# Moving the second ffn1's routing into the attention, and sorting its rows by expert with scatters from GpSimd

## The chip, the cores and the metric

The kernel runs on one core of a Trainium2 chip, as one program with one launch. The time is that of the device in microseconds, the median of several runs. TensorE's clock is granted at one of two levels, 1.2 and 2.4 GHz, and the profile gives it as a share of the higher.

## The reference

An activation `x` of 4 sequences of 1024 tokens and 128 features goes through six residual steps, each on a layernorm of `x`:

```python
x = x + 0.5 * L0_ffn(layernorm(x))     # shared GEGLU expert + the best of 8 experts
x = x + mamba(layernorm(x))            # 4 Mamba-2 experts, mixed by a softmax
x = x + 0.5 * L0_ffn(layernorm(x))
x = x + 0.5 * L1_ffn(layernorm(x))     # "ffn1"
x = x + attention(layernorm(x))        # causal, q and k of 16 features, v = the input
x = x + 0.5 * L1_ffn(layernorm(x))     # "ffn1" again, with the same weights

def L1_ffn(x):
    scores, experts = top_k(x @ Wg + bg, 2)          # of 8 experts
    gate = softmax(scores)
    # for each of the two: a = gelu(x @ W1[e] + b1[e]) (even e) or silu (odd e)
    return sum of gate * (a @ W2[e] + b2[e])
```

## The kernel before

**Layout.** The 4096 tokens are 32 tiles of 128 (token `t*128 + p` on partition `p`), 8 groups of 4 tiles. `x` stays in SBUF. Each stage is a block with one program for each engine, and engines wait for each other by semaphores; every engine runs its program strictly in the written order. A block ends when all engines have ended.

**An ffn1 stage** has a routing and an expert pass. `route` (L381) finds the two best experts of all tokens with VectorE instructions over 256 scores a partition, counts each expert's tokens with two matmuls, and gives every pair of token and choice a position: the experts one behind the other, each rounded up to whole slots of 128 rows, 71 slots at most (`SLOTS2`). Then 16 batches (`match_vector`, `match_lanes`, `match_tiles`, `place_tensor`) invert this by one-hot products, so that `slot_token` says for each row of a slot which token it holds, and `slot_row` where its result goes. `experts` (L771) then runs the 71 slots. For slot `s`: GpSimd gathers its 128 rows from `xn_rows` in DRAM (`gather`, L816, an indirect DMA); TensorE turns them (`turn`, L849); ScalarE copies them and the expert's W1 (L895, L890); TensorE multiplies (`up`, L861), VectorE adds the bias (L941), ScalarE and VectorE apply gelu or silu (L907, L910, L951), TensorE multiplies again (`down`, L873), and VectorE adds the bias and writes `y` (L964).

What happens to `y` differs. In the first ffn1 (`by_token`) SyncE stores the slots in order (L836), and the attention fetches the rows by position. In the second, GpSimd scatters each slot's rows into `y_rows` by token (`scatter`, L822), in the same program as the gathers, eight slots behind; VectorE's next `y` in that buffer (4 of them) waits for it. At the end SyncE brings `y_rows` back, VectorE adds the rows with their gates to `x`, and the output is stored (L280, L300).

**The attention** (`attend`, L1003) handles 32 blocks of 128 queries. Step `n` of its hand-written loop has, on each engine, the pieces of several blocks: TensorE scores block n, turns the probabilities of n-2 and mixes n-3; VectorE adds n-4 to `x` and finds the maximum of n; ScalarE copies the turned n-2 and takes the exponential of n. Woven in by tables from step to group: GpSimd fetches (`fetch`, L1111) the first ffn1's rows of a group, 8 gathers; VectorE adds them (`take`, L1160) and takes statistics (L1168, L1172, for group 5 in step 15); GpSimd makes the scale and shift (`deviations`, L1101 to L1107), ScalarE norms (L1324, group 5 in step 16); then turns, projections to q and k. Behind the blocks, the same for the second ffn1: once a group's four blocks are added, in step 4g+7, VectorE's `next_statistics` (L1180, L1184), GpSimd's `next_deviations` (L1129 to L1135), ScalarE's norm in step 4g+9 (L1346), turn, copy, scores and `logits`, and SyncE's store to `xn_rows` (L1089). GpSimd's program is, for g = 1 to 7: half the fetch of group g+1, `deviations(g)`, from g = 3 on `next_deviations(g-3)`, the other half of the fetch; the last three `next_deviations` behind it.

## Time and profile before

| | |
|---|---|
| median of 3 runs | 1868.59 us (1867.08 to 1868.68) |
| span of the profiled execution (first to last instruction) | 1864.5 us |
| the profiled execution's own time | not given apart from its span; what lies around a span is 4.1 us against the median |
| TensorE, VectorE, GpSimd, ScalarE busy | 1538, 1227, 1068, 953 us |
| mean granted TensorE clock | 0.906 |

Engines are named PE (TensorE matmul), PEld (TensorE weight load), DVE (VectorE), ACT (ScalarE), POOL (GpSimd) and SP (SyncE); a name with a q is that engine's sequencer. L816 is line 816 of the kernel before. All positions in time are us from the span's start. "Busy" says that an instruction was under way, not that it bounded anything. Idle time in brackets stands behind the instruction that ended it, with what released it.

### The profile page before, as it was taken

The page shows a single profiled execution, that of the slowest core. Times are in us where ns is not written, and L with a number is a line of the kernel's source. Part 1 is how long each engine was busy: PE and PEld are TensorE (multiplying, and loading weights), DVE is VectorE, ACT ScalarE, POOL GpSimd, SP SyncE. Part 2 cuts the span into 40 slices and gives each one's busy share as a digit, 9 for nine tenths or more (in the row PEclk, how much of TensorE's full clock was granted, in tenths as well). Part 3 has the DMA queues.
Part 4 walks back from the last instruction along what each step waited for, and adds up shares of the span by engine and source line. Part 5 has one row for each costly group of instructions (what it writes and reads, how often), then busy time and mean ns, then how long its engine had stood idle before and what let it go on. Part 6 is the DMA issues. An engine that isn't in the chain of part 4 may idle for free. (4 is left out here: it accounts for less than half of the span.)

```text
span 1864.5 us, 35936 instructions
## 1 busy us (share of the span) xinstructions
PE 1538.4 (83%) x10014; PEld 1275.6 (68%) x10015; DVE 1227.0 (66%) x2746; ACT 952.5 (51%) x1962; POOL 1067.6 (57%) x1408
## 2 busy tenths in 40 slices
PE   5879965799999999999869889646995588469883
PEld 3559962478888888888746589635995367358772
DVE  5535547689899999998655445575675477654556
ACT  2213343687878787877622223334663466345451
POOL 2135751388888888888840347535442563267773
PEclk9999966899999999999979999857998698679997
DMA  7001130000000000000031001421221110011115
GB/s 243 1 23 32 46 104 29 2 3 3 3 2 3 3 3 3 2 3 2 2 131 67 17 26 47 136 79 43 65 65 43 33 47 27 18 30 51 49 49 158
DMA packets 66072, 78.88 MB, mean 42 GB/s; under 512 B 23776, under 2 KB 40448, under 8 KB 65936
## 3 DMA queue, kind: packets, MB, share of 16 engines
q1 hardware_dynamic: 51952, 48.82, 8.4%
q0 software_dynamic: 13856, 28.40, 5.7%
q8 instruction: 64, 1.05, 0.2%
q14 instruction: 72, 0.59, 0.1%
q10 hardware_dynamic: 128, 0.02, 0.0%
HBM read 50.20 MB, written 24.90 MB: 40 GB/s over the span
## 5 line engine op out<-in xcount | busy, mean ns | idle before, releaser
L861 PE MATMUL ps<-gT,w_slot 128*128 128x128 f32 x1760 | 246.2, 284 | 4.0 <-ACT gT L895 2.8
L816 POOL DMA_INDIRECT rows_in<-xn_rows,slot_token x188 | 186.0, 989 | 110.1 <-PE ps L849 57.2
L873 PE MATMUL ps<-w,inner_slot 128*128 x1760 | 235.3, 277 | 2.4 <-DVE inner_slot L951 1.8
L861 PEld LDWEIGHTS ps<-gT,w_slot 128*128 128x128 f32 x1760 | 219.9, 196 | 17.7 <-issue 7.9
L822 POOL DMA_INDIRECT y_rows<-y,slot_row x149 | 162.1, 1088 | 108.5 <-DVE y L958 84.9
L873 PEld LDWEIGHTS ps<-w,inner_slot 128*128 128x128 f32 x1760 | 213.9, 192 | 6.7 <-issue 5.0
L1828 DVE SCALAR_TENSOR_TENSOR xbc<-ps,cw,xbc 128x1021 f32<-128x1021 f32 x132 | 168.2, 1274 | 17.8 <-ACT xbc L1707 15.7
L1582 PE MATMUL ps<-xnT,win 128*128 128x512 f32 x256 | 135.0, 653 | 26.3 <-DVE xbc L1828 21.0
L941 DVE TENSOR_TENSOR hb<-ps,b 128x512 f32<-128x512 f32 x142 | 98.1, 691 | 72.0 <-PE ps L861 66.4
L489 POOL TENSOR_TENSOR oh_slot<-match,tile_of 128x284 bf16<-128x284 bf16 (+1 forms) x48 | 46.5, 969 | 171.0 <-DVE match L470 171.0
L2010 POOL TENSOR_TENSOR xd<-t,xd 128x256 f32<-128x256 f32 x128 | 94.6, 739 | 86.9 <-DVE t L1863 86.9
L1633 PEld LDWEIGHTS ps<-XB,LM 128*128 128x128 f32 x1024 | 136.2, 194 | 6.8
L1633 PE MATMUL ps<-XB,LM 128*128 128x64 f32 x1024 | 129.7, 270 | 0.0
L1843 DVE SCALAR_TENSOR_TENSOR LM<-LM,past 128x512 f32<-128x512 f32 x128 | 122.7, 959 | 0.1
L1989 POOL TENSOR_TENSOR Xw<-XB,wst 128x256 f32<-128x256 f32 x128 | 89.8, 702 | 57.4 <-ACT XB L1748 57.4
L747 ACT ACTIVATE gl<-ps 128x512 f32<-128x512 f32 x64 | 38.2, 597 | 148.7 <-PE ps L701 148.7
L2015 POOL TENSOR_TENSOR y<-xd,sz 128x256 f32<-128x256 f32 x128 | 106.1, 829 | 10.0
L900 ACT ACTIVATE gl<-ps 128x512 f32<-128x512 f32 x78 | 46.6, 597 | 124.4 <-PE ps L865 124.4
L849 PE MATMUL ps<-ident,rows_in 128*128 128x128 f32 x220 | 64.6, 295 | 46.2 <-DMA rows_in<-xn_rows,slot_token 33.9
L1648 PEld LDWEIGHTS ps<-wout,yT 128*128 128x128 f32 x512 | 74.2, 198 | 31.4 <-issue 25.4
L964 DVE TENSOR_TENSOR y<-ps,b 128x128 f32<-128x128 f32 x142 | 41.1, 289 | 81.6 <-DMA y_rows<-y,slot_row 50.3
L1582 PEld LDWEIGHTS ps<-xnT,win 128*128 128x128 f32 x256 | 46.4, 201 | 68.2 <-issue 38.5
(295 smaller groups left out, 3983.0 us busy)
## 6 DMA issues: line engine op xcount, KB each, us to landing
w<-in_L_ffn_W SPq DMA_DIRECT2D x5, 2048.0 KB, 11.4
xn_rows<-xn SPq DMA_DIRECT2D x24, 256.0 KB, 3.4
xn<-y_rows SPq DMA_DIRECT2D x24, 256.0 KB, 4.9
y_rows<-y SPq DMA_DIRECT2D x71, 64.0 KB
rows_in<-xn_rows,slot_token POOLq DMA_INDIRECT x220, 2.6
y_rows<-y,slot_row POOLq DMA_INDIRECT x149, 2.4
right<-rows SPq DMA_DIRECT2D x128, 3.0 KB
xn_rows<-rows SPq DMA_DIRECT2D x8, 256.0 KB, 2.0
```

The costliest lines, as they stand in the source:

```text
L816: nc.gpsimd.indirect_dma_start(k.rows_in[:, q, :], None, k.xn_rows[:, :], bass.IndirectOffsetOnAxis(ap=k.slot_token[:, s:s + 1], axis=0)). ...
L822: nc.gpsimd.indirect_dma_start(kept, bass.IndirectOffsetOnAxis(ap=k.slot_row[:, s:s + 1], axis=0), k.y[:, s % RING, :], None).then_inc(sto ...
L861: ins = nc.tensor.matmul(h1[:, u, b * P:(b + 1) * P], w[:, b * P:(b + 1) * P], k.gT[:, r, :], start=True, stop=True)
L873: ins = nc.tensor.matmul(py[:, q % 2, :], k.inner_slot[:, q % RING, b * P:(b + 1) * P], w_dn[:, ds(e * (FB * D) + b * D, D)], start=(b == ...
L941: V.tensor_tensor(k.hb[:, q, :].rearrange("p (b t) -> p b t", b=FB), h1[:, q, :].rearrange("p (b t) -> p b t", b=FB), bcast(k.b1[:, ds(e * ...
L1582: ins = nc.tensor.matmul(piece(n)[:, half * 512:(half + 1) * 512], m.win[:, e, ZW + blk * P:ZW + (blk + 1) * P], k.xnT[:, seq * SEQ + half ...
L1633: ins = nc.tensor.matmul(bankY[:, hd], M[:, r, h * P:(h + 1) * P], XB[:, x, hd], start=True, stop=True)
L1828: inc(V.scalar_tensor_tensor(out, piece(n)[:, 0:SEQ - back], m.cw[:, c, i:i + 1], out, ALU.mult, ALU.add), tap_done if i < 2 else a["conv"])
L1843: inc(V.scalar_tensor_tensor(heads(M[:, r, :]), heads(L[:, u % 3, :]), LARGE, bcast(past[:, r, :], 1, MH), ALU.min, ALU.mult), b["M"])
L1989: inc(G.tensor_tensor(heads(Xw[:, r, :]), heads(XB[:, u % 4, 0:ZW]), bcast(m.wst[:, c:c + MH], 2, HD), ALU.mult), b["Xw"])
L2010: inc(G.tensor_tensor(xd[:, u % 2, :], t2[:, u % 2, :], xd[:, u % 2, :], ALU.add), b["summed"])
L2015: inc(G.tensor_tensor(y2[:, u % 8, :], xd[:, u % 2, :], sz[:, u % 8, :], ALU.mult), b["y2"])
```

## The change

The routing of the second ffn1 is done group by group inside the attention. The group's scores stay in PSUM; VectorE picks the two experts (`choose`, table CHOOSE, step 4g+13), TensorE counts (`next_ranks`, step 4g+14), VectorE turns the counts into positions (`take_ranks`, `place`, step 4g+15). A position now lies in a region of 4096 rows that each expert has in `sorted_rows`, a new DRAM tensor of 33,792 rows with 129 elements (516 bytes): the normed row, and the number of the row in `y_rows` where its result goes. GpSimd writes the rows with 64 scatters (`send`, 8 for each group); its program in the attention is written out anew. The slot table (expert and first row of each slot) is made by `slot_table` at the end of the attention, with the gates. Rows of a slot that no token fills must hold valid targets: Mamba's SyncE program fills the whole tensor with blank rows beforehand, in 33 transfers.

The second expert pass has no routing and no gathers. SyncE loads slot `s` with one transfer of 128 rows that lie one behind the other, whose start it reads into a register, into one of 16 buffers; up to four loads are under way. The scatter of `y` takes its targets from the last column of the loaded rows. The first ffn1 keeps its routing, with one cast in place of four for the slot table.

```diff
-    for shift in range(4):
-        do(V.tensor_copy(k.slot_expert[:, shift, shift:shift + slots], k.erow[:, 0:slots]))
+    put_experts(k, do, slots)
+def put_experts(k, do, slots):
+    four = k.slot_expert[:, :].rearrange("p (a w) -> p a w", a=4)
+    do(k.nc.vector.tensor_copy(four[:, :, 0:slots], bcast(k.erow[:, 0:slots], 1, 4)))
...
-    RING, LAG, AHEAD, LEADS = 4, 4, 16 if top == 1 else 8, 8
-    gathered = [k.counter(f"slot_gathered{r}", 16, lead=0) for r in range(AHEAD)]
-    stored = [k.counter(f"slot_kept{r}" if by_token else f"slot_stored{r}", 16, lead=0) for r in range(RING)]
+    RING, LAG, AHEAD, LEADS = 4, 4, 16 if top == 1 or sorted_in else 8, 8
+    CALLS = 4 if sorted_in else AHEAD
+    gathered = [k.counter(f"slot_moved{r}" if sorted_in else f"slot_gathered{r}", 16, lead=0) for r in range(CALLS)]
+    stored = [k.counter(f"slot_moved{r}" if by_token else f"slot_stored{r}", 16, lead=0) for r in range(RING)]
...
+                row = k.rows_in[:, s % AHEAD, D:D + 1].bitcast(U32) if sorted_in else k.slot_row[:, s:s + 1]
+                nc.gpsimd.indirect_dma_start(kept, bass.IndirectOffsetOnAxis(ap=row, axis=0),
...
-                if early <= t < slots:
+                if early <= t < slots and not sorted_in:
...
+            if sorted_in:
+                for s in range(slots):
+                    if s >= CALLS:
+                        sp.wait_ge(transposed.sem, transposed.at(s - CALLS + 1))
+                    if s >= AHEAD:
+                        sp.wait_ge(stored[s % RING].sem, stored[s % RING].at((s - AHEAD) // RING + 1))
+                    first = sp.value_load(k.slot_base[0:1, s:s + 1], min_val=0, max_val=SORTED - P)
+                    sp.dma_start(k.rows_in[:, s % AHEAD, :], k.sorted_rows[ds(first, P), :]
+                                 ).then_inc(gathered[s % CALLS].sem, 16)
...
+                pe.wait_ge(gathered[q % CALLS].sem, gathered[q % CALLS].at(n * (AHEAD // CALLS) + q // CALLS + 1))
...
-        NORM2, ROWS2, SCORE2 = ({n + back: g for n, g in AGAIN.items()} for back in (2, 4, 5))
-        END = 4 * NG + 9
+        NORM2, ROWS2, SCORE2, CHOOSE, RANK, PLACE = ({n + back: g for n, g in AGAIN.items()} for back in (2, 4, 5, 6, 7, 8))
+        END = 4 * NG + 12
...
-                for g in range(NG):
-                    wait(sp, next_xn, g + 1)
-                    sp.dma_start(xn_rows[:, g * GRP:(g + 1) * GRP, :], rows2[:, g % 2]).then_inc(next_stored[g % 2].sem, 16)
-                for r in range(2):
-                    wait(sp, next_stored[r], NG // 2)
...
-                for g in range(1, NG):
-                    if g + 1 < NG:
-                        fetch(g + 1, 0)
-                    deviations(g)
-                    if g >= 3:
-                        next_deviations(g - 3)
-                    if g + 1 < NG:
-                        fetch(g + 1, 1)
-                for g in range(NG - 3, NG):
-                    next_deviations(g)
+                def send(g):
+                    wait(pool, labelled, 1)
+                    wait(pool, index_ready, g + 1)
+                    wait(pool, next_xn, g + 1)
+                    for c in range(2):
+                        for j in range(GRP):
+                            G.indirect_dma_start(k.sorted_rows[:, :], bass.IndirectOffsetOnAxis(ap=index[:, g, c, j:j + 1], axis=0),
+                                                 back[:, g, c, j, :], None).then_inc(sent.sem, 16)
+                def fetch_group(g):
+                    fetch(g, 0)
+                    fetch(g, 1)
+                fetch_group(2)
+                deviations(1)
+                fetch_group(3)
+                fetch(4, 0)
+                deviations(2)
+                fetch(4, 1)
+                fetch_group(5)
+                deviations(3)
+                next_deviations(0)
+                fetch_group(6)
+                deviations(4)
+                next_deviations(1)
+                send(0)
+                deviations(5)
+                next_deviations(2)
+                fetch_group(7)
+                deviations(6)
+                next_deviations(3)
+                send(1)
+                deviations(7)
+                next_deviations(4)
+                send(2)
+                next_deviations(5)
+                send(3)
+                next_deviations(6)
+                send(4)
+                next_deviations(7)
+                send(5)
+                send(6)
+                send(7)
+                wait(pool, sent, NG * 2 * GRP)
...
+                def top_expert(c):
+                    do(V.tensor_reduce(best[:, c, :], lg[:, c], AX.X, ALU.max))
+                    do(V.tensor_tensor(eq[:, :, :], lg[:, c], bcast(best[:, c, :], 2, NE), ALU.is_equal))
+                    do(V.tensor_tensor(eq[:, :, :], eq[:, :, :], bcast(k.falling[:, :], 1, GRP), ALU.mult))
+                    do(V.tensor_reduce(low[:, :], eq[:, :, :], AX.X, ALU.max))
+                    do(V.tensor_tensor(sel[:, c], eq[:, :, :], bcast(low[:, :], 2, NE), ALU.is_equal))
+                def take_scores(g):
+                    wait(dve, next_scored, g + 1)
+                    V.tensor_tensor(lg[:, 0], ps_next.rearrange("p (j e) -> p j e", e=NE), bcast(k.bg[:, :], 1, GRP), ALU.add
+                                    ).then_inc(next_kept.sem, 1)
+                def choose(g):
+                    wait(dve, next_kept, g + 1)
+                    top_expert(0)
+                    do(V.scalar_tensor_tensor(lg[:, 1], sel[:, 0], -1e30, lg[:, 0], ALU.mult, ALU.add))
+                    top_expert(1)
+                    V.tensor_tensor(marks[:, 0:GRP, :], sel[:, 0], sel[:, 1], ALU.add).then_inc(marks_ready.sem, 1)
+                    V.tensor_sub(k.small[:, g * GRP:(g + 1) * GRP], best[:, 1, :], best[:, 0, :]).then_inc(weights.sem, 1)
+                def take_ranks(g):
+                    first = k.region if g == 0 else filled
+                    wait(dve, ranked, g + 1)
+                    wait(dve, placed, g)
+                    do(V.tensor_tensor(rank[:, :, :], ranks[:, 0:GRP, :], bcast(first[:, :], 1, GRP), ALU.add))
+                    V.tensor_tensor(filled[:, :], ranks[:, GRP, :], first[:, :], ALU.add).then_inc(placed.sem, 1)
+                def place(g):
+                    do(V.tensor_tensor(chosen[:, :, :, :], sel[:, :, :, :], bcast(rank[:, :, :], 1, 2), ALU.mult))
+                    do(V.tensor_reduce(posf[:, :, :], chosen[:, :, :, :], AX.X, ALU.add))
+                    V.tensor_copy(index[:, g], posf[:, :, :]).then_inc(index_ready.sem, 1)
+                def slot_table():
+                    slots, starts = SLOTS2, k.e8[:, 1, 1:NE]
+                    wait(dve, placed, NG)
+                    do(V.scalar_tensor_tensor(k.n_int[:, :], filled[:, :], float(P - 1), k.region[:, :], ALU.add, ALU.subtract))
...
+                    do(V.tensor_tensor(over[:, :, :], bcast(k.iota[:, 0:slots], 2, NE - 1), bcast(starts, 1, slots), ALU.is_ge))
+                    do(V.tensor_reduce(k.erow[:, 0:slots], over[:, :, :], AX.X, ALU.add))
+                    do(V.tensor_tensor(over[:, :, :], over[:, :, :], bcast(gap[:, 0:NE - 1], 1, slots), ALU.mult))
+                    put_experts(k, do, slots)
+                    do(V.tensor_reduce(k.erow[:, 0:slots], over[:, :, :], AX.X, ALU.add))
+                    do(V.scalar_tensor_tensor(k.slot_base[:, 0:slots], k.iota[:, 0:slots], float(P), k.erow[:, 0:slots],
+                                              ALU.mult, ALU.add))
...
-                for n in range(N + MIX + 1):
-                    if n > MIX:
+                for n in range(END):
+                    if MIX < n <= N + MIX:
                         add(n - MIX - 1)
+                    if group_behind(CHOOSE, n) is not None:
+                        take_scores(group_behind(CHOOSE, n))
+                    if group_behind(PLACE, n) is not None:
+                        take_ranks(group_behind(PLACE, n))
...
+                    if group_behind(PLACE, n) is not None:
+                        place(group_behind(PLACE, n))
+                    if group_behind(CHOOSE, n) is not None:
+                        choose(group_behind(CHOOSE, n))
                 wait(dve, added, N)
+                slot_table()
+                gates()
...
+                def next_ranks(n, g):
+                    wait(pe, marks_ready, g + 1)
+                    wait(pe, added, min(n - MIX, N))
+                    nc.tensor.matmul(ps_rank, k.before[:, :], marks[:, :, :].rearrange("p j e -> p (j e)"), start=True,
+                                     stop=False, skip_group_check=True)
+                    for j in range(GRP):
+                        ins = nc.tensor.matmul(ranks[:, j + 1:, :], k.ones_bf[:, :], bcast(marks[:, j, :], 1, GRP - j),
+                                               start=False, stop=(j == GRP - 1), skip_group_check=True)
+                    ins.then_inc(ranked.sem, 1)
...
+                    wait(pe, next_kept, len([m for m in SCORE2 if m < n + MIX]))
+                    wait(pe, placed, len([m for m in RANK if m < n + MIX]))
...
-                    wait(act, next_stored[r], g // 2)
-                    wait(act, next_turned, g - 1)
                     for j in range(GRP):
                         t = g * GRP + j
-                        ins = A.activation(rows2[:, r, j, :], x[:, t * D:(t + 1) * D], ACT.Identity,
+                        ins = A.activation(back[:, g, :, j, 0:D], bcast(x[:, t * D:(t + 1) * D], 1, 2), ACT.Identity,
...
+            def blank_rows(n):
+                e = n * 8 // NT
+                src = bcast(blank[:, e, :], 1, 8) if e < NE - 1 else blank[:, NE - 1:, :]
+                sp.dma_start(blanks[:, n * 8:(n + 1) * 8, :], src).then_inc(blank_in.sem, 16)
...
                 exponent_rows(n)
+                blank_rows(n)
+            blank_rows(NQ)
...
+SORTED = NE * TOK + 8 * P
...
+def ffn1_second(k, S, out):
+    ffn1_buffers(k, S, 16, D + 1)
+    experts(k, 2, SLOTS2, out=out, sorted_in=True)
```

## Rows read from the trace of the kernel before

**Rows 1.** the page's busy times, share of the span and number of instructions

```profile
PE 1538.4 (83%) x10014; PEld 1275.6 (68%) x10015; DVE 1227.0 (66%) x2746; ACT 952.5 (51%) x1962; POOL 1067.6 (57%) x1408
```

**Rows 2.** stretch table by stage: us, each engine busy, clock, DMA

```profile
290.00:1198.00 908.00, 831.29 (x5106) 671.91 (x5104) 686.49 (x1296) 548.20 (x1056) 595.96 (x843) 0.96 0.06 20
...
1274.00:1430.00 156.00, 145.32 (x1207) 138.94 (x1207) 90.54 (x179) 95.73 (x215) 68.41 (x71) 0.97 0.23 60
1430.00:1606.00 176.00, 120.33 (x674) 92.83 (x674) 100.51 (x386) 91.73 (x203) 88.59 (x131) 0.82 0.13 37
1606.00:1650.00 44.00, 10.82 (x67) 6.24 (x67) 40.53 (x89) 9.16 (x18) 16.64 (x16) 0.50 0.00 0
1650.00:1838.00 188.00, 163.28 (x1207) 142.65 (x1207) 91.95 (x178) 95.95 (x215) 143.37 (x142) 0.98 0.17 50
```

**Rows 3.** waits in the second pass: who waited for whom, us, times, longest

```profile
DVE y L964 <- DMA y_rows<-y,slot_row: 50.3, 51, 1.6
```

**Rows 4.** GpSimd in order of time, second pass: start, duration

```profile
1800.03 0.99 POOL L822 DMA_INDIRECT y_rows<-y,slot_row  x1 [0.30 <-issue]
1801.32 0.97 POOL L816 DMA_INDIRECT rows_in<-xn_rows,slot_token  x1 [0.31 <-issue]
```

**Rows 5.** turns and outputs, first pass, then second: min/median/max ns, first and last

```profile
L849 PE MATMUL ps<-ident,rows_in x71: 272/273/476, 1276.9 to 1418.6; 128*128 128x128 f32 x71
...
L964 DVE TENSOR_TENSOR y<-ps,b x71: 281/290/293, 1286.2 to 1426.1; 128x128 f32<-128x128 f32 x71
...
L849 PE MATMUL ps<-ident,rows_in x71: 272/328/476, 1653.0 to 1828.2; 128*128 128x128 f32 x71
...
L964 DVE TENSOR_TENSOR y<-ps,b x71: 282/291/293, 1661.9 to 1835.5; 128x128 f32<-128x128 f32 x71
```

**Rows 6.** all engines in order of time, routing's end to first turn

```profile
1648.67 0.23 DVE L514 TENSOR_TENSOR slot_row<-erow,rt 128x71 uint32<-128x71 f32 x1
...
1650.35 1.07 POOL L816 DMA_INDIRECT rows_in<-xn_rows,slot_token  x1 [6.46 <-POOLq L88]
...
1652.97 0.48 PE L849 MATMUL ps<-ident,rows_in 128*128 128x128 f32 x1 [8.30 <-DMA rows_in<-xn_rows,slot_token]
```

**Rows 7.** GpSimd in order of time, end of the second pass

```profile
1831.01 0.97 POOL L822 DMA_INDIRECT y_rows<-y,slot_row  x1 [0.30 <-issue]
```

**Rows 8.** the line that reads an expert's number into a register

```profile
L802 PEldq TENSOR_LOAD <-slot_expert x48: 297/364/1129, 141.9 to 1833.3; - x48
```

**Rows 9.** the page's DMA issues: KB each, us from issue to landing

```profile
y_rows<-y,slot_row POOLq DMA_INDIRECT x149, 2.4
...
xn_rows<-rows SPq DMA_DIRECT2D x8, 256.0 KB, 2.0
```

**Rows 10.** VectorE in order of time: last statistics of groups 2, 7; routing step

```profile
1528.78 0.38 DVE L1184 BATCH_NORM_AGGREGATE mv<-stat 128x2 f32<-128x6 f32 x4
...
1597.52 0.38 DVE L1184 BATCH_NORM_AGGREGATE mv<-stat 128x2 f32<-128x6 f32 x4
...
1616.48 0.17 DVE L345 CAST e<-n_int 128x8 f32<-128x8 int32 x1
```

**Rows 11.** the attention's 64 fetches on GpSimd: ns min/median/max

```profile
L1111 POOL DMA_INDIRECT back<-y_rows,pos x64: 940/944/1086, 1431.1 to 1551.6; - x64
```

**Rows 12.** GpSimd in order of time: first and last of two chains of deviations

```profile
1528.07 0.20 POOL L1101 TENSOR_TENSOR rstd<-mv,eps 128x4 f32<-128x4 f32 x1 [2.67 <-DVE mv L1172]
...
1531.64 0.23 POOL L1135 TENSOR_SCALAR shift<-shift 128x4 f32<-128x4 f32 x1
```

**Rows 13.** ScalarE in order of time: the norm of group 5

```profile
1531.83 1.64 ACT L1324 ACTIVATE xn<-x,shift,rstd 128x128 f32<-128x128 f32 x4
```

**Rows 14.** stretch table, blocks of the attention

```profile
1500.00:1600.00 100.00, 86.14 (x548) 69.81 (x547) 67.24 (x268) 66.89 (x152) 45.04 (x72) 0.95 0.13 38
```

**Rows 15.** the casts of the slot table

```profile
L374 DVE CAST slot_expert<-erow x4: 197/198/198, 1645.9 to 1646.6; 128x71 int32<-128x71 f32 x4
```

**Rows 16.** SyncE's issues in Mamba, in order of time

```profile
331.01 2.94 SPq L1966 DMA_DIRECT2D right<-rows  x4
```

More of the change, by code:

```diff
@@ L802, in fetch @@
             _, held = nc.values_load_multi_w_load_instructions(
-                k.slot_expert[0:1, shift, ds(t - behind + shift, count)], engines=(engine,), min_val=0, max_val=NE - 1,
+                k.slot_expert[0:1, ds(shift * WIDE + (t - behind + shift), count)], engines=(engine,), min_val=0, max_val=NE - 1,
                 skip_runtime_bounds_check_because="the table counts the experts whose first slot lies before a slot")
@@ L991, in experts @@
         biased.close(slots)
-    for q in range(AHEAD):
-        gathered[q].close((slots - q + AHEAD - 1) // AHEAD)
+    for q in range(CALLS):
+        gathered[q].close((slots - q + CALLS - 1) // CALLS)
     for q in range(RING):
@@ L1056, in attend @@
         ps_o, ps_p = k.ps[:, 6, 0:D], k.ps[:, 7, :]
+        ps_rank, ps_next = k.ps[:, 6, D:D + (GRP + 1) * NE], k.ps[:, 6, 2 * D:2 * D + GRP * NE]
+        ranks = ps_rank.rearrange("p (j e) -> p j e", e=NE)
         def block_of(n):
@@ new lines, in gates @@
+                def gates():
+                    wait(dve, gates_exp, 1)
+                    do(V.tensor_scalar(k.small[:, NT:2 * NT], k.small[:, 0:NT], 1.0, None, ALU.add))
+                    do(V.reciprocal(k.gate[:, 0, :], k.small[:, NT:2 * NT]))
+                    do(V.tensor_scalar(k.gate[:, 0, :], k.gate[:, 0, :], 0.5, None, ALU.mult))
+                    do(V.tensor_mul(k.gate[:, 1, :], k.small[:, 0:NT], k.gate[:, 0, :]))
+                V.memset(marks[:, GRP, :], 0.0).then_inc(zeros.sem, 1)
@@ L1213, in _ @@
+                V.tensor_copy(back[:, :, :, :, D].bitcast(I32), k.dest[:, :].rearrange("p (c g j) -> p g c j", c=2, g=NG)
+                              ).then_inc(labelled.sem, 1)
                 V.memset(kT[HALF:, :], 0.0).then_inc(zeros.sem, 1)
@@ L1236, in rows @@
                     wait(pe, qk_ready, g)
-                    wait(pe, next_kept, g - 3)
+                    wait(pe, next_copied, g - 3)
                     for j in range(GRP):
@@ L1265, in score @@
                     if n == 0:
-                        wait(pe, zeros, 1)
+                        wait(pe, zeros, 2)
                     wait(pe, expd, n - 1)
@@ L1303, in _ @@
                         turn(n - TURN)
+                    if group_behind(SCORE2, n) is not None:
+                        next_scores(n, group_behind(SCORE2, n))
+                    if group_behind(RANK, n) is not None:
+                        next_ranks(n, group_behind(RANK, n))
                     if 0 <= n - MIX < N:
@@ L1352, in next_copy @@
                     A.copy(xnT[:, g * GRP * P:(g + 1) * GRP * P], ps_p).then_inc(next_copied.sem, 1)
-                def next_keep(g):
-                    wait(act, next_scored, g + 1)
-                    A.copy(k.logits[:, g * GRP * NE:(g + 1) * GRP * NE], ps_p[:, 0:GRP * NE]).then_inc(next_kept.sem, 1)
                 def exponential(n):
@@ L1401, in _ @@
                         next_copy(group_behind(ROWS2, n))
-                    if group_behind(SCORE2, n) is not None:
-                        next_keep(group_behind(SCORE2, n))
+                wait(act, weights, NG)
+                A.activation(k.small[:, 0:NT], k.small[:, 0:NT], ACT.Exp).then_inc(gates_exp.sem, 1)
         weights_in.close(len(loads))
         bias_in.close(len(biases))
-        for s in (next_stat, next_var, next_rstd, next_xn, next_turned, next_copied, next_scored, next_kept):
+        for s in (next_stat, next_var, next_rstd, next_xn, next_turned, next_copied, next_scored, next_kept, marks_ready,
+                  ranked, placed, index_ready, weights):
             s.close(NG)
-        for s in next_stored:
-            s.close(NG // 2)
+        sent.close(NG * 2 * GRP)
+        labelled.close(1)
+        gates_exp.close(1)
+        route_own.close(k.route_steps)
         next_pool.close(3 * NG)
@@ L2046, in _ @@
             do(G.memset(m.left0[SUMS:SUMS + 32, :], 1.0))
+            do(G.memset(blank[:, :, :], 0.0))
+            do(G.iota(blank[:, :, D].bitcast(I32), pattern=[[P, NE + 7]], base=2 * TOK, channel_multiplier=1))
             wait(pool, init, 1)
@@ L2221, in ffn1_weights, with ffn1_buffers, ffn1_first @@
     ]
-def ffn1_passes(k, S, by_token, scale, out=None):
+def ffn1_buffers(k, S, gathered, width):
+    k.rows_in, k.gT, k.w_slot = S("rows_in", [P, gathered, width]), S("gT", [P, 2, P]), S("w_slot", [P, 2, FF])
+    k.inner_slot, k.hb, k.y = S("inner_slot", [P, 4, FF]), S("hb", [P, 4, FF]), S("y", [P, 4, D])
+def ffn1_first(k, S):
     nc = k.nc
-    k.rows_in, k.gT, k.w_slot = S("rows_in", [P, 8, D]), S("gT", [P, 2, P]), S("w_slot", [P, 2, FF])
-    k.inner_slot, k.hb, k.y = S("inner_slot", [P, 4, FF]), S("hb", [P, 4, FF]), S("y", [P, 4, D])
+    ffn1_buffers(k, S, 8, D)
     done = k.counter("router_biased")
-    steps = 1 + (NE // 2 if scale else 0)
+    steps = 1 + NE // 2
     k.start()
```

71 lines of the change are left out of this document (46 added, 25 removed).

## Prediction

> **What bounds the kernel now.** I read the page's busy shares first. They only say that TensorE is the busiest engine over the whole span, at 83%, and that no engine is busy all the time [rows 1]. The change touches stages of quite different kinds, so the table of stretches comes next [rows 2]. It shows Mamba (908 us, TensorE busy 831), the first ffn1 expert pass (156 us, TensorE 145), the attention (176 us), the second routing (44 us, where TensorE is busy 11, and VectorE 41) and the second expert pass (188 us). The last two carry the same 71 slots as the first routing and pass, yet the second pass takes 32 us more.
>
> Then I read what the second pass waits for. VectorE's output waits 50.3 us in 51 pieces for the scatter of an earlier slot [rows 3]. The order in time shows why: GpSimd issues a scatter (0.99 us, then 0.3 of issue), a gather (0.97, then 0.3) and a scatter again, without a pause, 2.57 us for a slot [rows 4]. The first pass has gathers alone on GpSimd, because SyncE stores its rows in slot order. Its 71 turns go from 1276.9 to 1418.6, 2.02 us each, against 1653.0 to 1828.2, 2.50 us each, in the second [rows 5]. So GpSimd sets the second pass, and PE with its followers sets the first. Between the attention and the second pass nothing but routing runs: VectorE ends at 1648.90, GpSimd issues the first gather at 1650.35, and the first turn is at 1652.97 [rows 6].
>
> **The change part by part, the pass first.** The 71 gathers leave GpSimd, and SyncE loads each slot. GpSimd keeps the scatter alone, 0.97 + 0.30 = 1.27 us for a slot [rows 7], under the 2.02 us that the rest needs. From the first turn to the last y the first pass takes 1426.1 - 1276.9 = 149.2 us, the second 1835.5 - 1653.0 = 182.5 [rows 5]. The difference is 33.3 us, and I take it whole, because matmuls, copies and biases are those of the first pass, with as much indirect work left on GpSimd (one for each slot). Better than 2.02 us is bounded by weight loads: 138.94 us for 71 slots is 1.96 us each [rows 2], 4 us in all. The cost of the new loads is bounded below by nothing (hidden) and above by SyncE's own sequence. A register load takes 0.36 us, seldom 1.13 [rows 8], and a transfer from SyncE lands in 2.0 us [rows 9], in all some 2.4 to 3.5 us of latency. The wait on turn s-4 (the four counters) starts the load four slots, 8.1 us, before its turn, so it is hidden. The wait on the scatter 16 slots back ended long before.
>
> **The attention: work added to GpSimd.** 64 sends join the 64 fetches. A scatter of 128 rows of 512 B takes 1.27 us with its issue; I take that for rows of 516 B, 81.3 us. The new order of GpSimd's program decides when they run. The first send needs the positions of group 0, and they come in block 15, behind the second statistics of group 2, which end at 1529.2 [rows 10]. Until then GpSimd has time to spare; so the early sends don't start early. From there GpSimd has 64 sends (81.3), the fetch of group 7 (8 x 1.25 = 10.0 by [rows 11] with 0.3 of issue) and nine chains for deviations (two take 1528.07 to 1531.87, 1.9 each [rows 12], 17.1). That is 108.4 us. With 1.2 us for the positions and choices ahead of it, GpSimd would end at 1638.8 if it never waited.
>
> It does wait, and makes others wait. The eight sends of group 0 stand ahead of the deviations of group 5, whose statistics come in the same block 15. ScalarE's norm of group 5 started at 1531.83 without a wait [rows 13]. Now the deviations end at 1530.4 + 10.2 + 1.9 = 1542.5, 10.7 us later. Behind the norm in ScalarE's queue stand the copy of block 15 and the exponential of block 17, and for these wait TensorE's turns and mixes. ScalarE and TensorE are busy 67 and 86 of the 100 us from 1500 to 1600 [rows 14], so little is caught up: I take 9 us, with 0 and 12 as bounds. Later sends stand ahead of deviations with four blocks between, which is about what they take.
>
> VectorE gets 19 small instructions for each group (1 to take scores, 13 to choose, 2 for ranks, 3 to place). One takes 0.17 us [rows 10], and I count 0.20 with its chained wait, so 3.8 us a group and 19 us for the five groups that fall in the blocks up to 31. VectorE is idle 33 us of the 100 [rows 14]. Some fall into its waits and some delay a mix, so I take 5, bounds 0 and 19. ScalarE gives up its small copies of the logits, and doubles the width of its norms; TensorE gets five small bf16 matmuls a group. I take these as nothing: they lie beside the two terms above, and the removed waits for bank 7 pay for them.
>
> The end of GpSimd's work is then the later of two. One is 1638.8. The other starts with the last statistics, of group 7, which end at 1597.90 [rows 10]: + 9 + 5 + 1.9 for the deviations + 24 sends of groups 5 to 7 (30.5) = 1644.3. The last send lands 2.4 us after its start [rows 9], 1.1 beyond its slot: 1645.4. The change of block, 1.45 us as at 1648.90 to 1650.35 [rows 6], the register load (0.36) and the landing (2.0) put the first turn at 1649.2, 3.8 us ahead of 1652.97. So the 44 us of routing that disappear from VectorE's time come back almost whole as GpSimd's sends. The slot table and gates (some 25 instructions on VectorE) lie under sends 5 to 7.
>
> **The rest.** Four casts of 0.2 us [rows 15] become one in the first ffn1's routing; I take 0.4 us there, 0.9 being the upper bound. The 33 blank transfers (528 KB each) lie in Mamba's SyncE queue. SyncE issues four of a quad's five transfers in 2.9 us [rows 16], the next quad some 20 us later, DMA is busy 0.06 of that stage [rows 2], and they are fetched one quad ahead: nothing. Without that cover each of the 33 would cost its transfer; a 256 KB one lands in 2.0 [rows 9], so some 4 us each, 130 in all. The constants in setup and Mamba's start lie under input loads.
>
> **Sum:** 33.3 + 3.8 + 0.4 = 37.5 us off. The profiled execution has a span of 1864.5 us, so 1827.0; its own time is not shown apart from its span, and the median of the three runs is 4.1 above it. 1868.6 - 37.5 = 1831.
>
> **One rule that speaks against the change.** The 64 fetches take 940 to 1086 ns, with a median of 944, though VectorE worked beside them all through the attention [rows 11]. The Trainium skill, "SBUF — State Buffer", section "SBUF: two separate sides", says that while VectorE runs in a mode that takes the shared ports, GpSimd cannot write the descriptors of a DMA that it issues, and it has such a transfer go from about 620 to about 3100 ns. The trace does not agree for these instructions: none of the 64 is longer than 1.09 us. By that rule the sends would cost up to five times as much.
>
> **Rivals.** *Sends that cost more (the other side).* Rows of 516 B that start off a round address, and more VectorE work beside them, might lengthen a send. Sends come last in the chain, so all that they gain counts 24 to 64 times. The gain is used up when a send costs 37.5 / 64 = 0.6 us more, 1.85 us instead of 1.27. At twice the price it is 81 - 37 = 44 us slower, some 1912. For it: no transfer with such rows is in the trace. Against: scatter and gather differ by 0.05 us only [rows 4]. That mechanism is the one which the page on SBUF describes, with VectorE's ports as the cause. Chance 0.06.
>
> *The attention stretches.* The stall (12) and VectorE's steps (19) fall on the path in full, so 17 us more than I took: first turn 1666, time 1848. A part of it gives the times between. For it: VectorE is busy 67 of 100 and every mix waits for its addition. Chance 0.18 for 1838 to 1848.
>
> *The second pass keeps its pace.* If SyncE's sequence (wait, register load, transfer) or y's scatter set 2.50 us again, the change doesn't do what it says: only the 4.2 us are left, 1864. Against: the load has 8.1 us. Chance 0.05.
>
> *More is hidden.* The stall and steps cost nothing, GpSimd ends at 1638.8 (first turn 1643.7, 9.3 off) and slots reach 1.96 us (4 more): 47 off, 1822. Chance 0.11.
>
> **How the numbers follow.** My forecast, 1824 to 1838, has 0.60. The range goes from the case in which more is hidden, 1822, to the stretched attention, 1847; outside are most of the dear sends and of the kept pace, and the edges. Within 0.2% (3.7 us) is about what a measurement of this kernel can tell from no change. The dear sends end slower (0.06), half of the kept pace within the bound (0.02), and all else faster (0.92).
>
> **What will show it.** The profile after should have the second pass's turns 2.0 us apart with VectorE's output no longer waiting for a scatter, no stretch with VectorE alone after the attention, GpSimd issuing sends of 1.0 us until about 1645, ScalarE's norm of group 5 waiting some 10 us for GpSimd, and a first turn near 1649. The prediction is wrong if a send is far from 1.27 us, if the loads of slots arrive late, or if the attention blocks spread by more than 14 us.

## The result

The kernel after takes 1845.83 us (median of 4 runs, 1841.05 to 1846.47), the one before 1867.84 (4 runs, 1864.78 to 1868.68). The ratio is 0.9889, with a 95% interval of 0.9874 to 0.9903. That is 22.0 us less, where the prediction had 37.5 less. The direction was right. But 1845.8 lies outside the forecast of 1824 to 1838. It falls among the times that the prediction gave to its rival of a stretched attention (1838 to 1848), and largely for another reason, as the profile shows. The profiled execution took 1845.43 us with a span of 1843.7.

Here is the stretch table of the kernel after, cut at its own stages, with the columns of [rows 2]:

```profile
1274.00:1430.00 156.00, 144.35 (x1207) 138.14 (x1207) 90.53 (x179) 95.73 (x215) 68.48 (x72) 0.97 0.23 60
1430.00:1616.00 186.00, 123.29 (x688) 93.07 (x688) 118.22 (x495) 91.67 (x190) 124.97 (x166) 0.81 0.13 37
1616.00:1651.00 35.00, 4.24 (x28) 3.48 (x27) 13.07 (x61) 2.89 (x6) 26.45 (x30) 0.54 0.14 48
1651.00:1662.00 11.00, 0.00 (x0) 0.00 (x0) 0.00 (x0) 0.14 (x1) 0.00 (x0) 0.50 0.02 6
1664.00:1816.00 152.00, 144.73 (x1207) 138.25 (x1207) 90.08 (x178) 94.22 (x212) 67.10 (x71) 0.98 0.23 62
```

The last line is the second pass. It now looks like the first one in every column. The fourth line is new: 11 us in which no engine does anything. Next, the second pass's turns and outputs, as in [rows 5], and what GpSimd waited for from 1690 to 1780:

```profile
L866 PE MATMUL ps<-ident,rows_in x71: 272/273/476, 1664.8 to 1807.7; 128*128 128x128 f32 x71
```

```profile
L981 DVE TENSOR_TENSOR y<-ps,b x71: 281/291/293, 1673.3 to 1815.4; 128x128 f32<-128x128 f32 x71
```

```profile
POOL y_rows L830 <- DVE y L981: 48.3, 44, 1.7
```

The turns are 2.04 us apart (142.9 / 70). From the first turn to the last y it is 150.6 us, where [rows 5] gave 182.5, so 31.9 less. GpSimd now waits for VectorE's outputs, and VectorE's wait for a scatter [rows 3] is gone.

The first turn, however, is at 1664.8, which is 11.8 later than before. The account of the span is +11.8 (first turn), -31.9 (pass) and -0.7 (tail, 28.3 instead of 29.0), together -20.8, as measured (1864.5 to 1843.7).

What holds the first turn back is best seen in order of time, from the last send on (all engines):

```profile
1648.33 0.95 POOL L1164 DMA_INDIRECT sorted_rows<-back,index  x1 [0.30 <-issue]
1649.59 0.96 POOL L1164 DMA_INDIRECT sorted_rows<-back,index  x1 [0.31 <-issue]
1661.86 1.28 ACT L939 ACT_TABLE_LOAD   x1 [33.31 <-PEq L88]
1662.88 2.62 SPq L848 DMA_DIRECT2D rows_in<-sorted_rows  x3
...
1664.79 0.47 PE L866 MATMUL ps<-ident,rows_in 128*128 128x128 f32 x1 [36.22 <-DMA rows_in<-sorted_rows]
```

The last send ends at 1650.55 and lands at 1651.9 (2.3 us after its start). Nothing moves until 1661.86, and the page's groups of instructions don't say why, as they leave out what engines don't count as work. The line of the attention's block itself does, when it is asked for. L1108 is `with nc.Block()`, and its columns are duration in ns (min/median/max) and first and last start:

```profile
L1108 DVEq COMPARE_BRANCH  x1: 53/53/53, 1635.6 to 1635.6; - x1
L1108 DVEq DRAIN  x1: 17/17/17, 1635.9 to 1635.9; - x1
L1108 POOLq COMPARE_BRANCH  x1: 43/43/43, 1651.9 to 1651.9; - x1
L1108 POOLq DRAIN  x1: 9202/9202/9202, 1652.1 to 1652.1; - x1
```

VectorE was through with its program at 1635.6. GpSimd waited for the last landing until 1651.9, and then its DRAIN, the instruction that closes a block, ran from 1652.1 to 1661.3. The other engines' DRAINs take 7 to 342 ns. The kernel before had one too, of 5.6 us:

```profile
L1082 POOLq DRAIN  x1: 5579/5579/5579, 1599.6 to 1599.6; - x1
```

There it ended at 1605.2, under ScalarE's and TensorE's last work.

Ahead of the sends, in the middle of the attention, ScalarE shows the stall that the prediction had named, against [rows 13] (ScalarE in order of time):

```profile
1533.46 0.19 ACT L1501 ACTIVATION_READ_ACCUMULATOR probs<-ps,nmax 128x1 f32 x1
1543.61 1.65 ACT L1467 ACTIVATE xn<-x,shift,rstd 128x128 f32<-128x128 f32 x4 [9.96 <-POOL shift L1128]
```

The norm of group 5 starts at 1543.6 instead of 1531.83. The last statistics, those of the second norm of group 7, end late too. This is VectorE in order of time, to be read beside [rows 10]:

```profile
1615.98 0.38 DVE L1239 BATCH_NORM_AGGREGATE mv<-stat 128x2 f32<-128x6 f32 x4
```

They end at 1616.36, 18.5 us later than 1597.90, where the prediction had 14. So 15.6 us were missed at the first turn (1664.8 for 1649.2), in two places: about 6 up to the end of the last send (1650.55 for 1644.3), and about 9.3 between it and the first turn (14.2 for 4.9).

### The profile page after: what moved, and what is told of

Read it like the earlier page. It is cut to its first block and busy times, and to the rows that moved or that the text cites. A ratio compares the mean times of both kernels' runs of the same rounds, so it can differ in the third digit from the quotient of the medians.

```text
span 1843.7 us, 36305 instructions
## 1 busy us (share of the span) xinstructions
PE 1512.4 (82%) x9925; PEld 1268.9 (69%) x9988; DVE 1214.4 (66%) x2818; ACT 947.0 (51%) x1938; POOL 1040.6 (56%) x1389
## 3 DMA queue, kind: packets, MB, share of 16 engines
q1 hardware_dynamic: 95344, 68.86, 12.6%
## 5 line engine op out<-in xcount | busy, mean ns | idle before, releaser
L878 PE MATMUL ps<-gT,w_slot 128*128 128x128 f32 x1760 | 242.0, 282 | 5.7 <-ACT gT L912 2.5
L823 POOL DMA_INDIRECT rows_in<-xn_rows,slot_token x117 | 113.6, 971 | 81.4 <-PE ps L866 56.9
L1724 PE MATMUL ps<-xnT,win 128*128 128x512 f32 x256 | 135.3, 654 | 26.4 <-DVE xbc L1970 20.8
L830 POOL DMA_INDIRECT y_rows<-y,slot_row x78 | 91.1, 1167 | 86.7 <-DVE y L975 85.5
L830 POOL DMA_INDIRECT y_rows<-y,rows_in x71 | 68.0, 957 | 98.4 <-DVE y L981 98.1
L495 POOL TENSOR_TENSOR oh_slot<-match,tile_of 128x156 bf16<-128x156 bf16 (+1 forms) x32 | 29.9, 933 | 143.7 <-DVE match L476 143.7
```

The source lines that it names most:

```text
L823: nc.gpsimd.indirect_dma_start(k.rows_in[:, q, :], None, k.xn_rows[:, :], bass.IndirectOffsetOnAxis(ap=k.slot_token[:, s:s + 1], axis=0)). ...
L830: nc.gpsimd.indirect_dma_start(kept, bass.IndirectOffsetOnAxis(ap=row, axis=0), k.y[:, s % RING, :], None).then_inc(stored[s % RING].sem, 16)
L878: ins = nc.tensor.matmul(h1[:, u, b * P:(b + 1) * P], w[:, b * P:(b + 1) * P], k.gT[:, r, :], start=True, stop=True)
L1724: ins = nc.tensor.matmul(piece(n)[:, half * 512:(half + 1) * 512], m.win[:, e, ZW + blk * P:ZW + (blk + 1) * P], k.xnT[:, seq * SEQ + half ...
```

## Experiments

In all of them the times are compared with runs of the kernel before on the same chip. Each has one profiled execution. The attention starts at a point that differs by some microseconds from run to run (1426.1 to 1431.7 us, in e10 1419.1), so times inside it are counted from its first GpSimd instruction, the MEMSET of `bqk`: 1429.94 in the kernel after.

### GpSimd's DRAIN left out, once and with the next one

```diff
@@ attend            (e1 and e2)
-        with nc.Block() as block:
+        with nc.Block(no_gpsimd_drain=True) as block:
@@ Bench.start, the block of semaphore leads ahead of each stage    (e2 only)
-            with self.nc.Block() as block:
+            with self.nc.Block(no_gpsimd_drain=True) as block:
```

> The attention's block closes without GpSimd's DRAIN; all waits stay. Theory A, the DRAIN of 9.2 us (1652.1 to 1661.3) is what holds the second pass back and its price goes with it: first turn at 1655 to 1656 instead of 1664.8, time 1836 to 1838 against 1845.8. Theory B, the backlog that it works off is taken over by GpSimd's next DRAIN, the one that closes the small block of semaphore leads behind it: that one grows from 0.04 to about 9 us, time 1845 to 1846. Theory C, the boundary waits for something else (code of the next block, transfers) and the DRAIN only lies over it: no DRAIN is long, first turn still at 1664 to 1665, time 1845 to 1846.

> As the kernel without GpSimd's DRAIN at the attention's end, and the small blocks of semaphore leads close without it too. Theory A: the same 1836 to 1838 as with the one DRAIN gone, the small DRAINs being 0.04 us each. Theory B, the price moves to the next DRAIN: now it moves on to the second pass's own end, where GpSimd's DRAIN lies beside the last additions: 1836 to 1838 here and 1845 to 1846 with the one DRAIN gone. Theory C: 1845 to 1846.

With the one DRAIN left out: 1838.33 us against 1863.08 before, ratio 0.9883 (0.9864 to 0.9902), that of the kernel after. The line of the leads' block (L88) in this run:

```profile
L88 POOLq DRAIN  x1: 9202/9202/9202, 1645.2 to 1645.2; - x1
```

In the kernel after that DRAIN took 34 ns. It is now 9202 ns, to the nanosecond what the removed one had taken. With both left out: 1830.84 us, ratio 0.9839 (0.9823 to 0.9856), and the boundary looks so, all engines in order of time:

```profile
1644.23 0.95 POOL L1164 DMA_INDIRECT sorted_rows<-back,index  x1 [0.30 <-issue]
...
1647.45 1.28 ACT L939 ACT_TABLE_LOAD   x1 [24.23 <-PEq L88]
1648.48 17.13 SPq L848 DMA_DIRECT2D rows_in<-sorted_rows  x12
...
1650.28 0.47 PE L866 MATMUL ps<-ident,rows_in 128*128 128x128 f32 x1 [27.04 <-DMA rows_in<-sorted_rows]
```

From the end of the last send to the first turn it is now 5.1 us, against 14.2. The prediction had 4.9 for the whole boundary.

The expected times go back to the first measurement, in which the kernel before took 1867.84 us. Here it took 1863.08, so the ratios are what to compare. Theory A's 1836 to 1838 is 0.983 to 0.984 of 1867.84: e2 is there and e1 is not. So A falls, and C falls by the long DRAIN. Theory B holds as far as the next DRAIN: the price moves there, and the time is saved only when that one is left out too. Its last step, that the DRAIN behind the second pass then takes the price over, is not what the trace shows. That DRAIN, in the kernel after and in e2:

```profile
L816 POOLq DRAIN  x1: 7057/7057/7057, 1815.7 to 1815.7; - x1
```

```profile
L816 POOLq DRAIN  x1: 7067/7067/7067, 1800.9 to 1800.9; - x1
```

In the one it stands behind 71 scatters, in the other behind 199 indirect DMAs, and it takes the same. In e2 the 9.2 us appear in no later DRAIN of GpSimd's, and from the first turn to the span's end it is 178.4 us, against 178.9 in the kernel after. So past that point the price did not turn up again, and why is not shown.

### One DRAIN more, where GpSimd is idle

```diff
+                nc.gpsimd.drain()
                 send(0)
                 deviations(5)
```

> The kernel after, with one more GpSimd DRAIN ahead of the sends of group 0, where GpSimd sits idle for 15.2 us (1516.6 to 1531.7). 56 of the 128 indirect DMAs of the block are issued by then. Theory D, a DRAIN works off the indirect DMAs issued since the last one at some 0.07 to 0.08 us each (5.6 us before for 64, 9.2 us after for 128): the new one takes 4 to 5 us in the idle time, the last one falls from 9.2 to 5 to 6 us, time 1841.5 to 1842.5. Rival E, the DRAIN's price is set by the last DMAs and by the waiting for them, whatever came before: the last DRAIN stays at 9.2 us, time 1845 to 1847.

1839.86 us, ratio 0.9881 (0.9863 to 0.9899). The two DRAINs in the attention:

```profile
L1183 POOLq DRAIN  x1: 4926/4926/4926, 1512.4 to 1512.4; - x1
...
L1108 POOLq DRAIN  x1: 5942/5942/5942, 1645.4 to 1645.4; - x1
```

The last one fell from 9.20 to 5.94 us, as theory D has it, and rival E, in which it stays at 9.2, falls. With 128 indirect DMAs since the DRAIN before it takes 9.20, with 72 it takes 5.94, which is 58 ns for each of 56 and 1.75 us besides. For 64 that gives 5.48, and the kernel before took 5.58; for 56 it gives 5.01, and 4.93 was measured. The expected 70 to 80 ns were too high. From the last send's end to the first turn it is 10.9 us instead of 14.2, a gain of 3.3. The time itself does not resolve it: the interval overlaps that of the kernel after.

### The deviations of group 5 ahead of the first sends

```diff
-                send(0)
                 deviations(5)
+                send(0)
```

> deviations(5) ahead of send(0) in GpSimd's order, all else as after. Theory F, ScalarE's wait for the deviations of group 5 (norm 5 some 11 us late) carries through to the statistics of group 7 (1616.4 after, 1597.9 before) and to the end of the last send (1650.55): statistics of group 7 at 1605 to 1610, last send's end at 1640 to 1645, time 1836 to 1841. Rival G, GpSimd's own queue of sends is the bound from 1531.7 on and the wait only moves to a later group: statistics of group 7 within 3 us of 1616.4, time 1844 to 1847.

1838.67 us, ratio 0.9863 (0.9846 to 0.988). The norm of group 5 starts 103.6 us into the attention (1534.72 - 1431.13) instead of 113.7, so the stall is gone. The last statistics then end at 181.2, where the kernel after had 186.4 in two executions, and the last send at 214.5 instead of 220.6. The numbers fall between the two theories: the statistics end at 1612.3 (F 1605 to 1610, G from 1613.4 on), the last send at 1645.6 (F up to 1645), and the ratio's interval reaches into that of the kernel after. The stall does carry through, as F says, but in part: of 10 us some 5 reach those statistics, and 2 to 4 by the executions of e1, e3 and e2, which keep the stall and have 183.1, 183.2 and 184.9.

### The kernel after again, and both mendings together

e5 is the kernel after unchanged. e6 has the edits of e2 and of e4.

> The kernel after, unchanged, on the chip and beside the runs of the kernels below, so that they have it to be read against. Ratio to before 0.987 to 0.990 as first measured; from the last send's end to the first turn 14.2 us; the DRAIN 9.2 us.

> deviations(5) ahead of send(0), and both the attention's block and the small blocks of leads close without GpSimd's DRAIN. If the two prices are independent: 4 to 5 us (deviations first) and 9 to 9.5 us (DRAIN) off after, 13 to 15 together, ratio to before 0.981 to 0.983. Rival: with the DRAIN gone the earlier attention only waits for the sends, and the deviations' order brings under 1 us more than the DRAIN alone (ratio 0.9839 measured with it alone).

On one chip, beside 1862.51 before: the kernel after 1843.69 us, ratio 0.9891 (0.9875 to 0.9907), with 14.1 us from the last send's end to the first turn and again a DRAIN of 9202 ns. e6 takes 1831.11 us, ratio 0.9818 (0.9801 to 0.9834). That is 12.6 us below the kernel after, a little less than the 13 to 15 expected. The intervals of e6 and e2 overlap, so it is the profile that speaks against the rival: in e6 the last send ends 214.5 us into the attention, in the five executions with the stall at 216.7 to 220.6. So the gain of the order is still there when the DRAINs are gone, some 2 to 6 us.

### The choosing on VectorE done twice

```diff
                 def choose(g):
                     wait(dve, next_kept, g + 1)
+                    top_expert(0)
+                    do(V.scalar_tensor_tensor(lg[:, 1], sel[:, 0], -1e30, lg[:, 0], ALU.mult, ALU.add))
+                    top_expert(1)
                     top_expert(0)
```

> e6's kernel with VectorE's choosing of the two experts done twice over in each group: 12 more instructions of 0.19 to 0.23 us, 2.6 us a group, 21 us in all, same results. Theory H, VectorE's routing instructions stretch the attention about one for one: the statistics of group 7, counted from the attention's start, come 13 to 21 us later than in e6, time 10 to 21 us more. Theory I, they lie in VectorE's idle time and the stretch (13.6 us of the 18.5) comes from TensorE and ScalarE: the statistics of group 7 come at most 5 us later, time at most 6 us more.

1845.21 us, ratio 0.9902 (0.9887 to 0.9917), 14.1 us more than e6 on the same chip. The last statistics, in e6 and in e7, VectorE in order of time:

```profile
1611.93 0.38 DVE L1239 BATCH_NORM_AGGREGATE mv<-stat 128x2 f32<-128x6 f32 x4
```

```profile
1623.95 0.38 DVE L1239 BATCH_NORM_AGGREGATE mv<-stat 128x2 f32<-128x6 f32 x4
```

Counted from the attention's start (1431.66 and 1429.93) they end at 180.7 and 194.4. The trace has 11 more instructions a group, not the 12 expected, and a group's choosing takes 2.5 us longer. That is 20 us in all, 15 of them ahead of these statistics (six groups), and they lengthened this stretch by 13.7. Theory H holds at the lower end of what it gave, and I falls: these small instructions are on the path nearly in full, although VectorE is idle a quarter of the time (busy 76.8 of the 100 us from 1500 to 1600 in e6).

### The pass part of the change alone, on the kernel before

```diff
+    plain = top == 2 and not by_token
...
-                if early <= t < slots:
+                if early <= t < slots and not plain:
                     gather(t)
...
+            if plain:
+                for s in range(slots):
+                    if s >= AHEAD:
+                        sp.wait_ge(transposed.sem, transposed.at(s - AHEAD + 1))
+                    sp.dma_start(k.rows_in[:, s % AHEAD, :], k.xn_rows[(s % NT) * P:(s % NT + 1) * P, :]
+                                 ).then_inc(gathered[s % AHEAD].sem, 16)
```

> The kernel before, its route block and all, but its second pass loads 128 consecutive rows of xn_rows by a plain transfer from SyncE instead of GpSimd's gather of the slot's rows: the slots get other rows than the reference's, the work on them is the same. It shows the pass part of the change alone. Theory J, GpSimd's gather beside the scatter is all that paced the second pass: first turn to last y 150 to 152 us instead of 182.5, time 30 to 34 us below before, ratio 0.982 to 0.984, that is, further below than the whole change brings. Rival K, the pass gains only with sorted rows and the register loads or is bound by the scatters: under 20 us.

1830.88 us against 1862.51, ratio 0.9822 (0.9809 to 0.9836), 31.6 us less. Its turns in the second pass:

```profile
L856 PE MATMUL ps<-ident,rows_in x71: 272/273/472, 1652.7 to 1795.5; 128*128 128x128 f32 x71
```

They are 2.04 us apart, and the first one is where it was in [rows 6]. From the first turn to the last y it is 150.1 us. Theory J holds: with the gathers away from the scatters' engine the pass runs at the first one's pace, which is worth 31.6 us. The whole change brought 22.0 and, on this chip, 18.8 (1862.51 to 1843.69). So moving the routing into the attention cost 10 to 13 us in the kernel after, although it removed 44 us of VectorE's stretch.

### The last fetches earlier

```diff
+                fetch_group(7)
                 deviations(5)
                 send(0)
                 next_deviations(2)
-                fetch_group(7)
```

> e6's kernel with the 8 fetches of group 7 moved ahead of deviations(5), into the 12.7 us for which GpSimd sits idle there; no indirect DMA lies among the sends any more but the sends themselves. Theory L, GpSimd's queue as such bounds the attention's end: 8 x 1.26 = 10 us less between 1531 and the last send, last send's end 6 to 10 us earlier counted from the attention's start (214.8 in e6), time 6 to 10 us below e6, ratio 0.976 to 0.9785. Theory M, from group 2 on GpSimd waits for VectorE's indices and statistics (ready at 1570.5, 1585.9, 1601.1, 1612.7 in e6) and only the 24 sends behind next_deviations(7) bound the end: last send's end within 2 us of 214.8, ratio 0.9805 to 0.983.

1829.67 us against 1867.79, ratio 0.9788 (0.9767 to 0.9808). The ratio lies between the ranges of the two theories, and the intervals of e9 and e6 overlap, so the times don't part them. The profile does, as the last send ends 213.4 us into the attention, 1.0 earlier than in e6. GpSimd's 10 us of freed time became waits for VectorE (from 1534 to 1612: who waited, for whom, us, times, longest). In e6 this row is not there in that stretch; its one wait of 12.9 us lies ahead, where the fetches now are.

```profile
POOL rstd L1122 <- DVE mv L1227: 9.7, 2, 7.8
```

Theory M holds by the profile, for one execution of each: past the first groups GpSimd follows VectorE, and the end is next_deviations(7) and the 24 sends behind it.

### No DRAIN of GpSimd at all

e6 with `no_gpsimd_drain=True` in all nine blocks that the program has in its text, some of which it runs several times.

> e6's kernel with every block closed without GpSimd's DRAIN. Behind the attention nothing is left to gain; in the first layer's feed-forward the DRAIN behind 16 gathers (117.3 to 133.0, 1063.3 to 1078.8) ends 2 to 3 us after the last gather has left GpSimd, with TensorE idle for 6.7 and 4.7 us there. If those DRAINs set these two boundaries: 2 to 5 us each, 4 to 10 together, ratio to before 0.9765 to 0.9798. Rival: the slot loop there waits for its weights and gathers anyway: ratio within 0.9805 to 0.983, as e6.

1820.92 us against 1867.79, ratio 0.9751 (0.9731 to 0.9771), a little below the range expected. That is 8.8 us below e9, which ran beside it and has the other seven blocks' DRAINs, and 12.5 us below e6 with both ratios applied to 1867.8 (10.2 us as the times stand, on two chips). So the gain is at the upper end of the 4 to 10 expected, or over it. Against e9 the first turn of layer 0's first slot loop comes 5.6 us earlier (131.1 for 136.7), that of its second 10.2, that of the first ffn1 pass 12.3 (1266.1 for 1278.4), and the attention starts 11.7 earlier (1419.1 for 1430.8). The first turn of layer 0's second slot loop, TensorE in order of time, in e10 and then in e9:

```profile
1070.80 0.41 PE L866 MATMUL ps<-ident,rows_in 128*128 128x128 f32 x2 [1.49 <-PEq L572]
```

```profile
1080.97 0.52 PE L866 MATMUL ps<-ident,rows_in 128*128 128x128 f32 x2 [4.87 <-PEq L572]
```

TensorE's idle time there is 3.4 us shorter, and ahead of the first loop 3.5 (3.40 for 6.92). So these two boundaries give some 7 us, as the expectation had it, and its rival falls. The attention starts 11.7 us earlier; where the other 5 come from was not taken apart. This kernel is the fastest of all, 46.9 us below the one before.

## Why the prediction was right in direction and wrong in size

*The pass.* The term was 33.3 us. The profile shows 31.9 in its own stretch, and e8, with this part alone, 31.6 in the time. The register loads and the transfers on SyncE were hidden, as argued: from 1666 to 1812 TensorE waits for a load once, 0.7 us. The slots stay at 2.04 us each, 0.02 over the first pass.

*The change of block* is the step that failed, and the largest part of the miss. The prediction put it at "1.45 us as at 1648.90 to 1650.35", taken from a boundary where GpSimd had issued no DMA in the block that ended. Behind the attention's 128 indirect DMAs it has 9.2 us of DRAIN in it, and from the last send to the first turn 14.2 us pass. With both DRAINs left out, in e2, the end of the last send and the first turn are 5.1 us apart, against the 4.9 forecast. The nearest row would have been the attention's own end before, with its DRAIN of 5.58 us behind 64 fetches, which was covered by other engines. Without the 9.3 us the time would have been 1836.5, inside the forecast.

*The stall and VectorE's steps* were sized 9 and 5, and came out the other way round. Together they come to 18.9 us in the attention's own count (186.4 for 167.5, the end of the last statistics less the attention's start), against 14 forecast. The stall was as long as forecast (10.0 us on ScalarE, the norm 11.8 later), but only 2 to 6 us of it arrive at the last statistics (183.1 to 186.4 with it in e1, e3, e2, e5 and the kernel after, 180.7, 180.8 and 181.2 without it in e6, e10 and e4), so part of it is caught up. The granted clock of the stretch 1530 to 1560 was 0.94 before and 0.77 after, a mean between its levels of 1.2 and 2.4 GHz, with TensorE busy 26.9 and 18.6 of the 30 us; with the stall removed it was 0.87. The 13 to 14 us left (180.7 to 181.2 for 167.5) come with the work added to each group, where the prediction had 5, under its bound of 19. e7 shows that such VectorE instructions count nearly in full. How the 13 to 14 us are made up is not shown. The trace of the kernel after has 111 of the routing's instructions ahead of those statistics, 21 us busy, because six groups choose before them and not the five that the prediction counted; at e7's rate they would give more than was measured. TensorE's and ScalarE's changed work, which the prediction took as nothing, was not tried by itself. That VectorE is idle 33 of 100 us hid little. A likely reason, not tested, is that its instructions stand in a chain of attention blocks in which one engine waits for the other.

*The end of the sends.* A send cost 1.26 us, as taken (1.27), and the chain behind the last statistics took 34.2 us instead of 32.4. The rival of dear sends did not come true: the 64 took 954 to 1212 ns with VectorE at work beside them, so the rule of the Trainium skill that the prediction weighed ("SBUF — State Buffer", section "SBUF: two separate sides") did not show itself here either. Whether VectorE was ever in the mode that it names, no run here shows.

*The casts and the blank transfers.* The attention began 0.46 us earlier than before, the 0.4 that was forecast, though this start moves by several microseconds from run to run, so it is no proof. The 33 blank transfers landed in 4.7 us each (median), and Mamba did not become longer.

*The account.* Forecast and measurement of the profiled execution are 37.5 and 20.8 us off the span, so 16.7 apart: 9.3 in the change of block, 4.9 in the statistics of group 7 (18.9 for 14), 1.8 in the chain of sends behind them and 1.4 in the pass, less 0.7 that the tail gave. That the time fell among those of the stretched attention is in large part luck. This rival had the stall and the steps 17 us over the sum, and they came 4.9 over it; the 9.3 us of the DRAIN stood in no rival.

## What to carry to other kernels

A block boundary can have a price that depends on what the block did. Ask the profile for the line of the block itself, and look for GpSimd's DRAIN there: in the attention it grew with the indirect DMAs issued since the last one, other engines covered it until a change made GpSimd the last, and leaving it out did not help while the next one stood right behind it. A load taken off the engine that paces a loop is worth what the loop's twin shows, whereas small instructions added to VectorE's part of the attention counted nearly in full, though the engine was idle a quarter of the time. Where one change has a part that gains and a part that costs, run the gaining part alone: here it was worth more than the whole.

## What the runs showed of the hardware

In the attention GpSimd's DRAIN took 4.93, 5.58, 5.94 and 9.20 us behind 56, 64, 72 and 128 indirect DMAs, gathers, scatters or both, and the last of the 64 had been issued 47 us before it began. That is about 1.75 us and 58 ns for each. When the first DRAIN was left out, the same 9202 ns appeared in the one right behind it.

In the expert passes a DRAIN begins as the last DMA is issued, so there it is counted from that DMA's end. Behind 71 gathers (first pass) and behind 71 scatters (second pass after) it ended 5.9 us later, and behind 62 of both kinds (layer 0) 5.1; by the same sum it would be 5.9 and 5.3. Behind the 16 gathers at the end of layer 0's routing it is 2.3, for 2.7 by the sum. It is not the whole rule. Behind the 142 of the second pass before it ended 3.6 us after the last one, and behind the 199 in e2 (and again in e6, e7 and e9) 5.9 us, where the sum would give 10 and 13. No other DRAIN stands behind more than 128. What happens there was not tried.
